# Row maximum in two operations, and the values' remainder from ScalarE's copy, in an attention kernel with routed experts

## The reference, cut to what matters

```
h = h + attention(layernorm(h))      # 8 heads of 64, scores rounded to bf16, softmax over 113 keys
h = h + experts(layernorm(h))        # one shared expert, and the 3 best of 16 routed ones, weighted by sigmoid gates
```

```
scores = (q * scale) @ k.T           # per head 113 x 113, rounded to bf16
probs  = softmax(scores)             # needs the maximum of every row of 113
out    = probs @ v                   # v kept to nearly fp32
y      = out @ Wo + bo
```

## Time and profile before

| | us |
|---|---|
| median of 3 runs | 810.36 (809.16 to 811.22) |
| the profiled execution's own time | 811.83 |
| its span | 810.0 |
| busy: TensorE matmul / weight load | 631.4 / 532.1 |
| busy: VectorE | 586.3 |
| busy: GpSimd | 553.6 |
| busy: ScalarE | 437.6 |
| attention steps, first to last row maximum | 76.41 to 460.68 |
| TensorE's granted clock in the attention stage | 1.00 of 2.4 GHz |

### The profile page before, as it was taken

How to read it: one execution, slowest core, us unless ns; L and a number is a source line. 1 busy time by engine, 2 the same in 40 slices (tenths; PEclk the granted TensorE clock), 3 DMA queues, 4 the chain that set the end, 5 groups by cost and what they waited for, 6 DMA issues and landing times.

```text
span 810.0 us, 20105 instructions
## 1 busy us (share of the span) xinstructions
PE 631.4 (78%) x6122; PEld 532.1 (66%) x6122; DVE 586.3 (72%) x2030; ACT 437.6 (54%) x1044; POOL 553.6 (68%) x696
## 2 busy tenths in 40 slices
PE   6667899999999999999999679663999889872000
PEld 4445778888888888888888557542888677762000
DVE  0687899999999999999999937343566565653244
ACT  2546878888888888888887623211343233220000
POOL 4364122687878878787877877777577777777464
PEclk9977999999999999999999959967999999997555
DMA  9910000011111111011111245535666565881697
GB/s 315 262 34 19 1 3 1 25 34 33 33 34 33 33 34 33 30 33 36 31 34 33 85 123 149 150 118 164 200 200 197 182 194 175 247 270 35 172 337 223
DMA packets 66444, 88.02 MB, mean 109 GB/s; under 512 B 11612, under 2 KB 58848, under 8 KB 66186
## 3 DMA queue, kind: packets, MB, share of 16 engines
q1 hardware_dynamic: 30420, 34.76, 15.4%
q10 hardware_dynamic: 23824, 28.68, 12.1%
q0 software_dynamic: 12096, 23.30, 8.5%
HBM read 57.32 MB, written 30.87 MB: 109 GB/s over the span
## 4 chain that ended last, share of the span: by engine, by line
DVE 25%; PE 22%; issue 13%; POOL 10%; DMA 8%; ACT 6%; SPq 2%; ACTq 1%; DVEq 0%; POOLq 0%
POOL expert_rows L629 6%; DMA x2t<-expert_rows 4%; DMA expert_rows<-yb,dst_i 3%; PE bank L893 3%; DVE mx L1324 3%; PE bank L687 3%; PE bank L783 2%; POOL dispatched L610 2%; DVE s L1329 2%; DVE vr L1368 2%; PE bank L797 2%; PE bank L902 2%; ACT p L1020 2%; DVE st L1341 2%; DVE o L1362 1%
## 5 line engine op out<-in xcount | busy, mean ns | idle before, releaser
L610 POOL DMA_INDIRECT dispatched<-pay,sloti x192 | 200.2, 1043 | 53.5 <-issue 52.5
L629 POOL DMA_INDIRECT expert_rows<-yb,dst_i x186 | 182.0, 979 | 61.3 <-issue 48.9
L1054 ACT ACTIVATE xe<-bank 128x256 f32<-128x256 f32 x93 | 35.7, 384 | 156.6 <-PE bank L882 132.0
L687 PE MATMUL bank<-xt,wqkv 128*128 128x452 f32 x384 | 100.3, 391 | 7.1 <-issue 5.9
L1445 DVE TENSOR_TENSOR hide<-bank,sge 128x256 f32<-128x256 f32 x93 | 39.3, 422 | 69.4 <-ACT sge L1059 35.3
L687 PEld LDWEIGHTS bank<-xt,wqkv 128*128 128x128 f32 x384 | 67.9, 193 | 14.0 <-issue 8.0
L1324 DVE TENSOR_REDUCE mx<-s 113x8 bf16<-113x904 bf16 x64 | 69.7, 1089 | 2.1 <-ACT s L1026 1.7
L836 PE MATMUL bank<-kt,qt 64*113 64x113 f32 x1024 | 67.1, 270 | 5.1 <-DVE h L1339 5.1
L1455 DVE TENSOR_TENSOR yb<-bank,gd 128x256 f32<-128x256 f32 x93 | 38.9, 418 | 43.4 <-DMA expert_rows<-yb,dst_i 39.9
L893 PE MATMUL bank<-xe,kt 128*128 128x256 f32 (+1 forms) x296 | 66.8, 355 | 2.6 <-issue 2.4
L1026 ACT ACTIVATE s<-bank 113x452 bf16<-113x452 f32 x128 | 63.1, 550 | 5.9 <-PE bank L836 5.8
(11 more groups left out here) (209 smaller groups left out, 1743.3 us busy)
## 6 DMA issues: line engine op xcount, KB each, us to landing
kt<-in_w_ffn ACTq DMA_DIRECT2D x74, 192.0 KB
xs_all<-dispatched SPq DMA_DIRECT2D x77, 140.0 KB
x2t<-expert_rows SPq DMA_DIRECT2D x16, 672.0 KB
vr<-in_w_ffn ACTq DMA_DIRECT2D x35, 192.0 KB
out_h<-h ACTq DMA_DIRECT2D x16, 224.0 KB
x2t<-in_x ACTq DMA_DIRECT2D x4, 864.0 KB, 9.8
x2t<-in_x SPq DMA_DIRECT2D x4, 864.0 KB, 11.3
dispatched<-pay,sloti POOLq DMA_INDIRECT x192
```

The source lines that it names most:

```text
L610: pool.indirect_dma_start(out=xs_dram[:, :], out_offset=bass.IndirectOffsetOnAxis(ap=sloti[:, q % (PAYS // GRP), b, c:c + 1], axis=0), in_ ...
L629: pool.indirect_dma_start(out=y_dram[:, :], out_offset=bass.IndirectOffsetOnAxis(ap=dst_i[:, slot, j:j + 1], axis=0), in_=yb[t % RW][:, j, ...
L687: m = nc.tensor.matmul(dst, wqkv[:, a, at:at + 128], xg[:, b, :], start=(j == 0), stop=(j == 2))
```

## The change

The row maximum is made in two operations. The first takes the larger of columns 0 to 56 and columns 56 to 112 of each head, into a new tile `mh` of 8 x 57 bf16 numbers; it stands ahead of the second normalisation (L1319). The second reduces `mh`, behind it, and waits for the new semaphore `half_max`. Column 56 is in both halves.

The remainder `vr` is made from `vf` in memory instead of bank 1. TensorE waits for `v1_done` (ScalarE's copy) instead of `vr_done` before it reuses bank 1, in two places.

Point 1 of the routing moves from behind L1346 to between the residual add (L1339) and its statistics (L1341).

```diff
+        mh = sb("mh", [128, H, TP // 2], BF16)
...
-                    after(pe, "vr_done", n)
+                    after(pe, "v1_done", n)
                     after(pe, "q_copied", n + 4, 0)
                     project_t(bank[1][:, 0:GT], kk * 128, xt[1 - g]).then_inc(S["qa_done"], 1)
...
-                    after(pe, "q_copied", n + 4) if ok(n + 4) else after(pe, "vr_done", n)
+                    after(pe, "q_copied", n + 4) if ok(n + 4) else after(pe, "v1_done", n)
...
                     nc.vector.tensor_scalar(xn[i][0:T, :], row(n + 8), mean1[0:T, bass.ds(n + 8, 1)], rs1[0:T, bass.ds(n + 8, 1)],
                                             ALU.subtract, ALU.mult).then_inc(S["xn_ready"], 1)
+                if ok(n):
+
+                    after(dve, "s_copied", n)
+                    nc.vector.tensor_tensor(mh[0:T, :, :], s16[i][0:T, :, 0:TP // 2], s16[i][0:T, :, T - TP // 2:T],
+                                            ALU.max).then_inc(S["half_max"], 1)
                 if ok(n - 3):
                     after(dve, "rs2_done", n - 3)
...
                 if ok(n):
 
-                    after(dve, "s_copied", n)
-                    nc.vector.reduce_max(mx[i][0:T, :], s16[i][0:T, :, 0:T], AX.X).then_inc(S["max_done"], 1)
+                    after(dve, "half_max", n)
+                    nc.vector.reduce_max(mx[i][0:T, :], mh[0:T, :, :], AX.X).then_inc(S["max_done"], 1)
...
                     nc.vector.tensor_tensor(row(n - 2), bank[3][0:T, 0:D], row(n - 2), ALU.add).then_inc(S["h_done"], 1)
+                routing(o, k, 1)
+                if ok(n - 2):
+
                     after_all(dve, ("txt_in", 32), ("h_done", n - 2, 1))
                     nc.vector.bn_stats(st2[0:T, i, :], row(n - 2)).then_inc(S["st2_raw"], 1)
...
                     nc.vector.tensor_tensor(xt[g][:, 1, at], bank[0][:, 0:T], xt[g][:, 0, at].bitcast(FP32),
                                             ALU.subtract).then_inc(S["xl_copied"], 1)
-                routing(o, k, 1)
...
-                    nc.vector.tensor_tensor(vr[(k + 1) % 4][0:T, :, :], bank[1][0:T, :].rearrange("p (h d) -> p h d", h=H),
+                    nc.vector.tensor_tensor(vr[(k + 1) % 4][0:T, :, :], vf[(k + 1) % 4][0:T, :, 0:DH],
                                             v1[(k + 1) % 4][:, :, 0:DH], ALU.subtract).then_inc(S["vr_done"], 1)
```

More of the change, by code:

```diff
@@ L257, in build @@
             "st1_raw st1_done mean1_done ve1_done rs1_done xn_ready xt_done xt_copied qa_done qb_done q_copied k_copied "
-            "v_done v1_done vr_done v_ready "
+            "v_done v1_done vr_done v_ready half_max "
             "s_done s_copied max_done mx2_done sub_done exp_done pt_done pt_copied av_done rec_done o_ready ot_done ot_copied "
```

## The result

| | before | after |
|---|---|---|
| median of the runs | 810.79 (809.16 to 812.50, 4 runs) | 822.39 (819.15 to 823.93, 4 runs) |
| the profiled execution's own time | 811.83 | 822.95 |
| its span | 810.0 | 821.2 |

The ratio of the two is 1.0134, with a 95% interval of 1.0100 to 1.0167. The forecast was 803.7 us, with a range of 797.0 to 812.5; the time lies outside it, on the side of the rival that I gave 0.15.

The account below looks back on a forecast made before the run. VectorE was taken to lead now, GpSimd to set the step after the change. Savings of 4.5, 1.5 and 0.7 us took 811.8 to 805.1; the runs' median, 1.5 lower, made it 803.7 us, range 797 to 812.5.

Parts of the forecast that it names:

- What the new source does to GpSimd: Attention steps: the remainder read from memory delays scatters by 0.30 us, 0.19 comes back; net +0.11, GpSimd at 6.01 per step.
- Row maximum: VectorE's maximum in two operations: 0.81 us of engine time against 1.00 for the one, so -0.19 per step.
- Residual and statistics: VectorE's gap between residual add and statistics: the moved routing part fills 0.07 to 0.19 us, taken as 0.15 per step.
- TensorE's earlier reuse: TensorE's wait ahead of the first projection goes: 0.52 us in one step of four, next to nothing in the others.
- what is late next: After TensorE's earlier reuse of the bank, L746 is late next, still waiting for L1362 as before.
- The remainder's price on GpSimd: The remainder's second memory operand holds the scatter behind GpSimd's power: 0.30 us per step, net +0.11, bounds 0 and +0.30.
- The 0.19 given back: GpSimd's present delays shrink: a scatter loses 0.37 us less and L592 some 0.4 less, each in one step of four.
- GpSimd's 5.90: GpSimd's attention step if nothing slows it: 6.11 us less the 0.21 that it waits for VectorE.
- GpSimd takes it all: Rival, chance 0.19: the remainder holds no scatter that wouldn't have waited anyway; steps of 5.90 us, 12 us saved, 798 us.
- The gain is eaten: Rival, chance 0.20: GpSimd's delays of 0.2 us per step use up its idle time; step stays 6.1, about 809 us.
- Slower: Rival, chance 0.15: the remainder fully holds a scatter in three steps of four and GpSimd's power; 6.25 us per step, 816 us.

## Why the prediction was wrong

**The step that failed is "What the new source does to GpSimd".** It priced one of VectorE's two new instructions with two operands in memory and overlooked the other. The section on the row maximum took the new maximum's duration from L1329, "the same operation on the same tile", and the section on GpSimd used L1329 as an example of what holds a scatter; the one was never brought to the other. It also took the meetings with the old instructions to get rarer: the scatter held by the subtraction L1329, one in four steps, "should go", and it became one in every step (1.28 us in the mean where it was 0.975). The runs showed in its place: without the split GpSimd's work grows by 0.20 us a step, its spare time covers that, and the step is 6.09; with it, and the second operand gone, 6.19; with it whole, 6.37.

Point by point:

- *Row maximum*: 0.38 forecast for the maximum of halves, 0.40 where nothing disturbs it (399 ns in the mean of the version with split and point) and 0.42 in after; 0.61 forecast for the reduction, 0.62 measured. Of the 0.19 of VectorE's time 0.15 is there: between starts, the two take 0.32 and 0.54 in the version with split and point, against 1.00 for the one. Its worth isn't: nothing beyond the intervals without the source, a loss with it. L1329 isn't the same operation, as it subtracts, but its rate held. The Trainium skill, VectorE: DVE Perf Modes, section "Mode 2×_1P — pack two bf16 into one 32-bit read", asks for 4-byte alignment; by that the maximum would have taken 0.61. The trace doesn't bear it out: 0.399 for 456 results against 0.634 for the 912 of the subtraction in the same execution is 0.52 ns a result, half of the reduction's 1.06.
- *Residual and statistics*: the gap is gone, and the whole gain that any part of the change brought is here: 0.12 us a step where I took 0.15 for VectorE.
- *TensorE's earlier reuse*: the idle time ahead of the projection goes (after has none), and it is worth nothing, as "what is late next" is the attention output. That was said; that it takes back all of it wasn't.
- *The remainder's price on GpSimd*: without the split GpSimd's work grows by 0.20 a step where I had a net +0.11, inside the bounds, and GpSimd's pace is 6.08 (the step of 6.09 less 0.01 of waiting) in place of 6.01. But it was to hold the scatter behind the power by 0.30. Such a scatter began beside the remainder in 16 steps of 44, not in three of four, and took 1.46 to 1.49 in 8 of them; in the mean this scatter grew by 0.10. The power took 0.19 more, which is the mechanism that I had given to the slower rival alone, and the second scatter 0.11 more. The 0.19 given back came out in size by luck: half of it was to come from a scatter, and nearly all of it came from L592 (0.18: 1.33 to 0.59 in one step of four).
- *GpSimd's 5.90*: it was taken as a pace with fixed durations. The durations hang on what VectorE does beside each instruction, and a faster VectorE changes all of these meetings at once.

The rivals: "GpSimd takes it all" would have needed a source that holds nothing. "The gain is eaten" is what source, wait and point without the split do (0.998, a step of 6.09). "Slower" named the right engine, the right wait (VectorE for the power) and the right sign, and stopped at 6.25 and 816 us, since it too knew only one holding instruction. The real step is 6.37.

That the forecast of 803.7 us equals the 803.7 to 804.4 us of the versions without the memory source is a coincidence of the sum: it had 0.19 from the split and took 0.11 off for the source.

## What to carry to other kernels

A VectorE instruction with two operands in memory had a second price here, paid by whatever GpSimd started beside it. Before such an instruction is added, or an operand moved from a bank to memory, look at where GpSimd's shortest instructions start: those that start beside it are stretched past its end, so that several short ones can lose more than one long one. Look at the old instructions too: with the reduction shorter and GpSimd later, the second scatter of every step stood beside a two-operand subtraction and no longer beside the reduction. If GpSimd has little waiting left, take work off it in the same change (0.14 us more on VectorE bought 0.48 us of the step here), and measure each part of a change by itself: one part here held all the gain that could be measured.

## What was not expected of the hardware

- The tail behind the holding instruction is fixed per kind: 0.30 to 0.32 us for an addition of 113x128, 0.05 to 0.09 for one of 113x1, 0.42 to 0.44 for the power of 113x1. A power that takes 0.57 us alone took 1.12 beside a whole remainder of 0.66.
- GpSimd holds VectorE in turn, beside an instruction with one operand in memory: in after the first normalisation L1314 takes 0.48 us in place of 0.34 in the ten steps in which a lengthened bias still runs for some 0.4 us beside it, and ends 0.08 to 0.09 behind the bias.
- Reductions, with one operand, held next to nothing: the power beside a reduction of 0.35 us took 0.587 in the mean, 0.718 beside a two-operand maximum of 0.42.
- The kernel before took 811 to 812 us in four comparisons and 908 and 920 in two, on other chips, and there source alone gave 0.9982 on the one and 0.9907 on the other. I haven't found out why. It isn't one stage alone: the attention step of split and point is 6.23 and 6.33 us there against 5.97, and TensorE's granted clock is 1.00 in these steps on all three.
